# Conditioned residual on one core: x and result laid out as on chip, 1 MB transfers, whole-bank moves, two loads ahead of the gather

## What is computed

```python
w = weights[conditions]                       # [64, 64, 64]: one 64x64 matrix per batch entry
out = x + jnp.einsum('bct,bcd->bdt', x, w)    # x: [64, 64, 512] fp32
```

## Time and profile before

| | us |
|---|---|
| median of 3 runs | 51.25 |
| lowest, highest | 50.74, 51.54 |
| the profiled execution, its own time | 50.88 |
| span of the profiled execution | 49.1 |
| busy: DVE, PE, ACT | 24.8, 17.5, 17.4 |

### The profile page before, as it was taken

How to read it: one execution, slowest core, us unless ns; L and a number is a source line. 1 busy time by engine, 2 the same in 40 slices (tenths; PEclk the granted TensorE clock), 3 DMA queues, 4 the chain that set the end, 5 groups by cost and what they waited for, 6 DMA issues and landing times.

```text
span 49.1 us, 383 instructions
## 1 busy us (share of the span) xinstructions
PE 17.5 (36%) x128; PEld 7.0 (14%) x128; DVE 24.8 (50%) x28; ACT 17.4 (35%) x17; POOL 1.6 (3%) x9
## 2 busy tenths in 40 slices
PE   0000000000000069997495959696969300000000
PEld 0000000000000023240333334343424000000000
DVE  1043000000089930059999999999999997000000
ACT  0720000000000000059977878796969690000000
POOL 4003500000000000000000000000000000000000
PEclk9999999999999999999999999999999999555555
DMA  0399999999999999999999999999999999999950
GB/s 0 68 382 406 350 361 334 417 409 429 386 397 401 386 389 384 389 386 391 382 389 392 411 404 402 414 407 404 407 411 406 404 404 406 404 406 412 402 199 13
DMA packets 8851, 17.84 MB, mean 364 GB/s; under 512 B 530, under 2 KB 530, under 8 KB 8722
## 3 DMA queue, kind: packets, MB, share of 16 engines
q1 hardware_dynamic: 8704, 16.78, 90.7%
q0 software_dynamic: 144, 1.05, 5.1%
q10 hardware_dynamic: 2, 0.00, 0.0%
HBM read 9.44 MB, written 8.39 MB: 363 GB/s over the span
## 4 chain that ended last, share of the span: by engine, by line
DVE 45%; DMA 19%; issue 8%; PE 8%; DVEq 3%; POOL 1%; POOLq 1%
DVE y_sb L152 37%; DMA gathered<-weights,table_row 19%; PE product L119 8%; DVE w_all L146 7%; DVEq L36 3%; POOL piece L101 1%; DVE gathered L143 1%; POOLq L36 0%; POOLq L161 0%
## 5 line engine op out<-in xcount | busy, mean ns | idle before, releaser
L119 PE MATMUL product<-x_sb,w_all 64*64 64x512 f32 x128 | 17.5, 669 | 21.0 <-DVE w_all L146 17.6
L95 ACT COPY y_sb<-product 64x1024 f32<-64x1024 f32 x16 | 16.1, 1007 | 21.7 <-PE product L119 21.5
L152 DVE COPY y_sb<-product 64x1024 f32<-64x1024 f32 x16 | 19.6, 1223 | 4.3 <-PE product L119 3.8
L119 PEld LDWEIGHTS product<-x_sb,w_all 64*64 64x64 f32 x128 | 7.0, 204 | 30.7 <-DVE w_all L146 17.6
L143 DVE TENSOR_TENSOR gathered<-gathered,piece 128x64 f32<-128x64 f32 x1 | 0.3, 268 | 9.4 <-DMA gathered<-weights,table_row 9.4
L146 DVE STREAM_TRANSPOSE w_all<-gathered 128x2048 f32<-128x2048 f32 x1 | 3.6, 3621 | 0.0
L95 ACT ACT_TABLE_LOAD x1 | 1.3, 1283 | 1.5 <-DVE condition L126 1.5
L133 DVE STREAM_TRANSPOSE condition_of<-condition 32x32 int32<-32x32 int32 x4 | 0.8, 202 | 1.8 <-DMA condition<-conditions 1.7
L103 POOL DMA_INDIRECT gathered<-weights,table_row x1 | 1.1, 1068 | 3.2 <-DVE table_row L137 3.2
L126 DVE MEMSET condition<- 32x64 int32 x1 | 0.1, 112 | 0.8 <-PEq L161 0.8
L101 POOL MEMSET piece<- 32x1 f32 x4 | 0.4, 91 | 0.5 <-POOLq L161 0.3
## 6 DMA issues: line engine op xcount, KB each, us to landing
x_sb<-x SPq DMA_DIRECT2D x16, 512.0 KB, 11.2
out<-y_sb SPq DMA_DIRECT2D x16, 512.0 KB, 5.8
condition<-conditions ACTq DMA_DIRECT2D x1, 0.2 KB
gathered<-weights,table_row POOLq DMA_INDIRECT x1, 9.1
```

The source lines that it names most:

```text
L95: nc.scalar.copy(y_sb[halves(0), slots_of(turn, g), :], product[turn % SETS][0][halves(g), :, :]).then_inc(moved_by_act, 1)
L119: product_of = nc.tensor.matmul(product[turn % SETS][h][halves(g), j, :], w_all[halves(h), :, n], x_sb[halves(h), n, :], start=True, stop= ...
L152: nc.vector.tensor_copy(y_sb[halves(1), slots_of(turn, g), :], product[turn % SETS][1][halves(g), :, :]).then_inc(moved_by_dve, 1)
```

## The change

x is handed to the kernel already in the order [partition, pair, time], the table already transposed within its 32x64 pieces, and the result is written in the order [partition, pair slot, time]; the host rearranges around the launch. A partition's part of four pairs is now 8 KB of unbroken memory, and SP issues 8 loads and 8 stores of 1 MB. The first two loads go out at once. Ahead of the third, SP waits for `gather_started`, a semaphore that POOL raises with its gather instruction. Each moving engine now takes both banks of one `product` tensor in one instruction, over all 128 partitions. PE waits for one load per turn instead of two. The transpose into `w_all` now reads `gathered` contiguously.

```diff
-            for m in range(ROUNDS):
-                sp.dma_start(x_sb[:, 2 * m:2 * m + 2, :], x_rows[:, 2 * m:2 * m + 2, :]).then_inc(x_loaded[m], 16)
-            for m in range(ROUNDS):
-                if m % 2 == 0:
-                    sp.wait_ge(moved_by_act, m + 2)
-                    sp.wait_ge(moved_by_dve, m + 2)
-                sp.dma_start(out_rows[:, 2 * m:2 * m + 2, :], y_sb[:, 2 * m:2 * m + 2, :]).then_inc(stored, 16)
-            sp.wait_ge(stored, 16 * ROUNDS)
+            for turn in range(TURNS):
+                if turn == EARLY:
+
+                    sp.wait_ge(gather_started, 1)
+                sp.dma_start(x_sb[:, pairs_of(turn), :], x[:, pairs_of(turn), :]).then_inc(x_loaded[turn], 16)
+            for turn in range(TURNS):
+                sp.wait_ge(moved_by_act, turn + 1)
+                sp.wait_ge(moved_by_dve, turn + 1)
+                sp.dma_start(out[:, pairs_of(turn), :], y_sb[:, pairs_of(turn), :]).then_inc(stored, 16)
+            sp.wait_ge(stored, 16 * TURNS)
...
-                for g in range(2):
-                    nc.scalar.copy(y_sb[halves(0), slots_of(turn, g), :], product[turn % SETS][0][halves(g), :, :]
-                                   ).then_inc(moved_by_act, 1)
+                nc.scalar.copy(y_sb[:, 4 * turn:4 * turn + 2, :], product[turn % SETS][0][:, :, :]
+                               ).then_inc(moved_by_act, 1)
...
-                                         ).then_inc(w_gathered, 16)
+                                         engine_sem=gather_started).then_inc(w_gathered, 16)
...
+                pe.wait_ge(x_loaded[turn], 16)
                 if turn >= SETS:
-                    pe.wait_ge(moved_by_act, 2 * (turn - SETS + 1))
-                    pe.wait_ge(moved_by_dve, 2 * (turn - SETS + 1))
+                    pe.wait_ge(moved_by_act, turn - SETS + 1)
+                    pe.wait_ge(moved_by_dve, turn - SETS + 1)
                 for j in range(2):
-                    pe.wait_ge(x_loaded[2 * turn + j], 16)
...
-            diagonal = bass.AP(gathered, 0, [[Q * D, P], [D + 1, Q], [Q, K]])
+            diagonal = bass.AP(gathered, 0, [[D * Q, P], [Q + 1, Q], [Q * Q, K]])
...
-            nc.vector.transpose(w_all[:, :, :], gathered[:, :].rearrange("p (c d) -> p d c", d=D)
+            nc.vector.transpose(w_all[:, :, :], gathered[:, :].rearrange("p (d c) -> p d c", d=D)
                                 ).then_inc(w_ready, 1)
 
             for turn in range(TURNS):
                 dve.wait_ge(multiplied, turn + 1)
-                for g in range(2):
-                    nc.vector.tensor_copy(y_sb[halves(1), slots_of(turn, g), :], product[turn % SETS][1][halves(g), :, :]
-                                          ).then_inc(moved_by_dve, 1)
+                nc.vector.tensor_copy(y_sb[:, 4 * turn + 2:4 * turn + 4, :], product[turn % SETS][1][:, :, :]
+                                      ).then_inc(moved_by_dve, 1)
```

More of the change, by code:

```diff
@@ L17, in conditioned_residual_kernel @@
     ALU = mybir.AluOpType
[L19 to L23, removed]
+    P, PAIRS, T = x.shape
+    B = conditions.shape[1]
+    C = D = P // PAIR
     Q = 32
     K = C // Q
-    ROUNDS = PAIRS // 2
-    TURNS = ROUNDS // 2
+    TURNS = PAIRS // 4
     SETS = 2
[L30 to L33, removed]
+    EARLY = 2
     ctx = ExitStack()
@@ L54, in conditioned_residual_kernel @@
                    for s in range(SETS)]
-        x_loaded = [semaphore(f"x_loaded{m}") for m in range(ROUNDS)]
+        x_loaded = [semaphore(f"x_loaded{turn}") for turn in range(TURNS)]
         condition_loaded = semaphore("condition_loaded")
```

28 lines of the change are left out of this document (18 added, 10 removed).

## The result

The changed kernel takes 49.1 us (48.59 to 49.29, 4 runs) against 51.2 before: ratio 0.960, 95% interval 0.949 to 0.972. Measured a second time, beside three of the experiments, it was 48.98 and 0.964 (0.958 to 0.971). Forecast: 48.8. The medians here are of all executions and the ratios leave out disturbed ones, so the two can differ: with 2 KB stores the ratio rests on two of six, and with all loads first only one was left and no ratio is given.

The account below looks back on a forecast made before the run. Bound taken: the rate of the DMA engines, not DVE. Loads -1.7, stores -0.9, wait +0.2 sum to -2.4: 50.88 becomes 48.5, plus 0.37 for the median, 48.8 us; 8 in 10: 47.5 to 50.9.

Parts of the forecast that it names:

- Loads: Loading x, 8.39 MB: from 390 GB/s to 424 with 8 KB packets, 21.5 to 19.8 us, -1.7 us.
- Stores: Storing the result: 20.7 us at 406 GB/s to 19.8 at 424, -0.9 us; bounds 0 and -1.1.
- The estimate from the Trainium skill: Loads and stores: about 3 fabric cycles overhead per packet, giving -1.4 us instead of -2.6; as a rival 50.0 us, 7%.
- The wait: SP's wait ahead of the third load: issue at 5.57, first byte 6.7, 2.10 MB queued until 6.8; charged +0.2 us.
- the signs of being wrong: Third load issued at 9 or at the gather's landing, a window under half busy, conditions after 3.5, stores still at 406.
- the third way: At the start: the conditions' load waits for the whole first 1 MB, everything to the semaphore 1.8 us later; 50.4 us.
- the dry-queue rival: Ahead of the third load: x's queue runs dry for about 2 us; three ways, together 24%, at about 50.5 us.
- its first byte follows 1.15 us later: Third load: issued at 5.57, flowing at 6.7, as the first load, issued at 0.76, flowed at 1.9.
- The rival with a semaphore at the landing: Third load: semaphore comes with the gather's landing, gather starts no earlier than now; +3.9 us, 52.5 us, 9%.
- The gather: Landing: 14.4 if started at 9 and sharing, 12.4 or before if started at 7; cost 0 up to 14.2.
- then a tail: End of the kernel: last part of the time, after the start and 17.84 MB at the DMA rate; no change charged.
- the slow stretch of the earlier trace: From 5 to 9 us at 352 GB/s, losing 0.4 us against later loads; left at 0, might vanish (-0.4).

Follow-up runs that it names:

- the 2 KB experiment: Changed kernel with x and the result laid out by pairs, so every load and store run is 2 KB again: 52.0 us, ratio 1.012.

## Why the prediction was right

The range and the direction held, and the time was met within 0.3 us of 48.8. The bound and the rates were right; that the whole came so close is in part luck, as two terms were wrong and others made up for them. The bound was read rightly: not DVE, to which the chain of waits pointed, but the rate of the DMA engines, which the windows showed.

*Loads*: forecast 424 GB/s and -1.7 us; measured 426, and 1.9 us by experiment. *Stores*: forecast 424 and -0.9; measured 429, -1.1 by rates. The gather's 8 KB packets were the right rows to price a packet size that the kernel did not yet use.

The estimate from the Trainium skill ("DMA: Bandwidth & Descriptors", "Why small descriptors are slow"), -1.4 for both, was too small: the 2 KB experiment costs (1.012 - 0.962) x 51.2 = 2.6 us with all else equal. The table of the same page of the Trainium skill (section "Bandwidth") has 425 GB/s for one load of 16 MB issued from GpSimd (POOL); the 426 of the loads here, issued by SP, agrees. The table has no stores.

*The wait*: forecast +0.2, and about 0.5 by the trace. This term was mis-sized, and its working failed in two steps. First, the semaphore came as forecast, with the end of the gather's record, but the record ended at 6.32 instead of 5.57, since the conditions' load reached DVE at 3.74 instead of 2.99. One of the signs of being wrong was a landing of the conditions after 3.5, and it came. The packet records show what made it late. The load's 256 bytes start at 3.08 instead of 2.56, and the 4 bytes that raise its semaphore 0.32 after them instead of 0.10, about one 8 KB packet instead of one of 2 KB. So it waited more than once, where I had charged one packet. It did not wait for the whole first megabyte, which was the third way of the dry-queue rival: 0.75 us, not 1.8.

Second, "its first byte follows 1.15 us later" was taken from the first load of an idle queue. The third load took 3.6 us from its issue to its first byte. With 1.15 it would have flowed at 7.5, just as the first two loads ran out, and the delay of 0.75 would have cost almost nothing. So x's queue did run dry, from 7.4 to 9.9 us, longer than the rival said. It cost little because the gather's packets were ready at 7.2 and filled the engines, where the rival had them idle. What was lost is the slow start of the gather: the window 7 to 9 ran at 291 GB/s, which is 2 x (428 - 291)/428 = 0.6 us; the trace with three early loads gives 0.5. Why a load takes 3.6 us to start there no run shows. The gather beside a filled queue is like it: with all loads first its record ends at 5.93 and its first packet starts at 9.05.

The rival with a semaphore at the landing is out; POOL's DRAIN again lasts until just past the landing (5.0 + 6.75), so a DRAIN's end does not tell when the semaphore is raised.

*The gather*: forecast to land at 12.4 or before if it started at 7; DVE went on at 11.70. *Moves and spacing*: forecast 0, and shown to be 0 by experiment. *Transfer size*: forecast 0; the rates with 2 KB runs don't move with it. *PE and the transpose*: forecast 0; PE is done 17 us before the end, and a gather 3.2 us later costs nothing, so nothing behind the gather was on the path. That a moving engine's time goes by elements per partition was left open and is now shown (1007 and 1015 ns for 64 and 128 partitions on ACT).

*What the sum did not contain*: one engine late at the end. The term "then a tail" was put at no change without a reason. It did change: about 0.2 us of the late engine showed in the kernel before, 0.8 in the changed one. On the other side the slow stretch of the earlier trace rows, 352 GB/s from 5 to 9 us, which I left as it was, is gone up to 7 us (430), worth up to 0.4. So: -1.9 - 1.1 + 0.6 + 0.6 - 0.4 = -2.2, against -1.8 to -2.1 measured. The dip at 24 to 26 us is not in this sum; its rate makes it 2 x (428 - 315)/428 = 0.5, which would give -1.7, though taking it away alone changed no time. The forecast's errors partly cancelled, which is luck: the rates and the slow stretch gave up to 0.8 more than forecast, the wait and the tail took 1.0.

## What to carry to other kernels

Where the DMA share stands at 1 from the first byte to the last, as here, doubt that an engine at nine tenths is the bound, however long its part in the chain of waits; price the change by bytes over rate, and take the rate from packets of the size that the change will use, in any queue that has them. A wait that lets one small transfer through early is to be judged by what the engines move meanwhile: here two early loads bought 3 us of landing time that nobody needed and cost 0.6 to 0.9. Take the time to the first byte from a transfer issued in the same state: an idle queue gave about 1.1 us, and a load issued while the engines were busy and a gather stood ready gave 3.6. And in a kernel that ends with a store over all engines, read the last microsecond engine by engine: here a share of 0.08 was one late engine.

## What the runs showed that was not expected

A PE program of 64 matmuls (256 records of matmuls and weight loads) brought one 16 KB packet on the instruction queue, at 28 to 39 us, in every trace; with 40 or 56 matmuls there was none. After it, in the traces with 8 KB loads, one DMA engine's part of every later store is late: 0.8 us on a kernel of 49. That the packet holds a part of PE's program is inferred from this, not seen. Where between 56 and 64 the limit lies was not tried.

The gather's packets of 8 KB took about 307 to 313 ns where they started beside loads of a filled queue, and 362 on average where the gather took over from an empty one; only the first ones were slow, 609 ns for those of the first microsecond. Why is open, as is why a load took 3.6 us to start, and why stores queued early slow the last load at 24 to 26 us.
